# Regrouping the TensorE transposes of a step in a paged-attention and LoRA kernel

## What is computed

```python
q, k, v = x @ Wq.T, x @ Wk.T, x @ Wv.T          # 4 query heads, 1 key and 1 value head in a group
q, k = rope(rmsnorm(q, q_norm_w)), rope(rmsnorm(k, k_norm_w))
k_all, v_all = concat(k_cache[pages], k), concat(v_cache[pages], v)      # 512 + 128 keys
scores = where(valid, q @ k_all.T / sqrt(128), -1e30)
x = x + (softmax(scores) @ v_all) @ Wo.T
base, h, logits = x @ W.T, x @ A.T, x @ Wr.T + language_bias
gates = softmax(top2(logits))                   # spread over the 8 experts
x = x + base + 2.0 * (h * gates) @ B
```

## Time and profile before

| | before |
|---|---|
| median of 3 runs | 1166.06 us (1165.09 to 1166.17) |
| the profiled execution's own time | 1164.94 us |
| its span | 1163.1 us |
| TensorE busy | 1144.9 us, 98% of the span |
| ScalarE, VectorE, GpSimd busy | 80%, 79%, 66% |
| DMA, mean | 84 GB/s |
| mean granted TensorE clock | 0.997 of full speed |

### The profile page before, as it was taken

The page is one execution under the profiler, slowest core; times in us unless marked ns, Lnnn a source line. Parts: engine busy times, 40 slices in busy tenths (PEclk is TensorE's granted clock), DMA queues, the critical chain, the costliest instruction groups (busy, mean ns, idle before and its releaser), DMA issues.

```text
span 1163.1 us, 20954 instructions
## 1 busy us (share of the span) xinstructions
PE 1144.9 (98%) x6932; PEld 1025.0 (88%) x6932; DVE 918.5 (79%) x1884; ACT 931.8 (80%) x1832; POOL 768.7 (66%) x833
## 2 busy tenths in 40 slices
PE   7899999999999999999999999999999999999998
PEld 6788888889989989988998998899899899889887
DVE  7988888787788778778778877877877787787746
ACT  6888888888888888888888888888888888887741
POOL 5766766767776676776677677677766767766600
PEclk9899999999999999999999999999999999999999
DMA  7423332223222223222322222222232222221001
GB/s 235 158 74 100 122 104 84 64 87 88 77 79 92 81 68 91 89 68 87 91 78 73 91 89 64 87 89 73 82 91 81 67 89 88 64 78 56 19 1 73
DMA packets 56763, 98.12 MB, mean 84 GB/s; under 512 B 8784, under 2 KB 29136, under 8 KB 56528
## 3 DMA queue, kind: packets, MB, share of 16 engines
q1 hardware_dynamic: 44368, 63.21, 17.2%
q0 software_dynamic: 12288, 33.57, 10.1%
HBM read 90.45 MB, written 6.29 MB: 83 GB/s over the span
## 4 chain that ended last, share of the span: by engine, by line
PE 92%; DVE 3%; ACT 2%; issue 1%; DMA 0%; POOL 0%; SPq 0%; ACTq 0%; DVEq 0%; POOLq 0%
PE ps_w L306 19%; PE ps_w L308 18%; PE ps_w L307 18%; PE ps_s L1297 18%; PE ps_w L1306 9%; PE ps_w L1375 2%; PE ps_w L1273 2%; PE ps_w L1280 2%; PE ps_s L1214 1%; ACT ps L645 1%; PE ps_w L1246 1%; DVE m L868 0%; DVE w_lo L792 0%; DVE pt_lo L792 0%; DMA w_raw<-wqkv 0%
## 5 line engine op out<-in xcount | busy, mean ns | idle before, releaser
L466 POOL DMA_INDIRECT kv_raw<-kv,rows x256 | 255.6, 999 | 95.7 <-issue 62.2
L651 ACT ACTIVATE ps<-ps,recip 128x640 f32<-128x640 f32 x256 | 213.1, 832 | 64.0 <-DVE recip L902 64.0
L792 DVE TENSOR_TENSOR pt_lo<-ps_w,pt_hi 128x512 fp32r<-128x512 f32 x322 | 210.3, 686 | 67.7 <-ACT pt_hi L656 65.3
L645 ACT ACTIVATE ps<-ps,negmax 128x640 f32<-128x640 f32 x256 | 211.6, 827 | 38.9 <-DVE negmax L895 38.9
L895 DVE CUSTOM_DVE_ANT_0 ps<-ps_s,mask 128x640 f32<-128x640 f32 x256 | 210.3, 822 | 7.5 <-PE ps_s L1297 3.5
L656 ACT ACTIVATE pt_hi<-ps_w 128x512 fp32r<-128x512 f32 x256 | 152.7, 596 | 57.2 <-PE ps_w L1306 57.2
L306 PE MATMUL ps_w<-w_hi,xt_hi 128*128 128x512 f32 (+1 forms) x496 | 177.0, 357 | 1.6 <-DVE w_lo L792 1.4
L308 PE MATMUL ps_w<-w_hi,xt_lo 128*128 128x512 f32 (+1 forms) x496 | 167.1, 337 | 0.0
L307 PE MATMUL ps_w<-w_lo,xt_hi 128*128 128x512 f32 (+1 forms) x496 | 166.7, 336 | 0.0
L1306 PE MATMUL ps_w<-cst,ps 128*128 128x128 f32 x1024 | 154.1, 273 | 1.0 <-DVE w_lo L792 0.8
L484 POOL TENSOR_TENSOR rot<-u,cos 128x640 f32<-128x640 f32 x63 | 100.5, 1596 | 69.4 <-DVE u L940 69.4
(11 more groups left out here) (182 smaller groups left out, 2598.6 us busy)
## 6 DMA issues: line engine op xcount, KB each, us to landing
xt_hi<-xsplit SPq DMA_DIRECT2D x56, 256.0 KB, 2.8
xt_lo<-xsplit SPq DMA_DIRECT2D x56, 256.0 KB, 2.8
w_raw<-wqkv SPq DMA_DIRECT2D x56, 192.0 KB, 2.4
wo_raw<-wo SPq DMA_DIRECT2D x56, 128.0 KB, 2.2
kv_raw<-kv,rows POOLq DMA_INDIRECT x256, 2.9
y<-xT SPq DMA_DIRECT2D x8, 256.0 KB, 3.6
y<-x SPq DMA_DIRECT2D x8, 256.0 KB, 5.6
out<-y SPq DMA_DIRECT2D x8, 256.0 KB, 2.2
```

The source lines that it names most:

```text
L466: pool.indirect_dma_start(kv_raw[:, g % 2, t, :], None, kv[:, :], bass.IndirectOffsetOnAxis(rows[:, g % B, t:t + 1], 0)).then_inc(s_kv[g % ...
L645: nc.scalar.activation(ps[:, h, :], ps[:, h, :], ACT.Exp, bias=negmax[:, s % 2, h:h + 1], scale=-1.0, accum_out=rowsum[:, s % 2, h:h + 1]) ...
L651: nc.scalar.activation(ps[:, h, :], ps[:, h, :], ACT.Copy, scale=recip[:, s % 2, h:h + 1]).then_inc(a_norm, 1)
L792: return nc.vector.tensor_tensor(out_ap, full, hi.bitcast(F32), ALU.subtract)
```

## The change

The order of TensorE in a step becomes: scores 0 and 1, query projection, scores 2, O, scores 3, then T0, T1, T2 in one run, Y, then QT, KTC, KTN, T3, TN in one run, and the key and value projection last, no longer cut in two. The eight banks are dealt out anew: the twelve uses of `ps_w` become eleven with a list for each bank, and KTN goes into the last 128 columns of a score bank. In the new lists KV stands behind QT, T3 behind T2, TN behind Y, KTC behind T1 and T0 behind Q. ScalarE and VectorE take their copies and low parts in the new order: the values ahead of T0; T2 ahead of the exponential of head 3 on ScalarE and ahead of its reciprocal on VectorE; the piece of the next weights ahead of QT; the piece of the output weights behind TN. In the first step and in the last ones the corresponding places are moved as well. No instruction is added or removed, apart from waits.

```diff
-UNITS = ["Q", "O", "T0", "T1", "Y", "T2", "QT", "KTC", "KV", "KTN", "T3", "TN"]
-NU = len(UNITS)
-NBANK = 4
+BANKS = (("Q", "T0", "QT", "KV"), ("O", "Y", "TN"), ("T1", "KTC"), ("T2", "T3"))
+NBANK = len(BANKS)
...
+        def new_keys_bank():
+            return ps_s[:, 1, 1, 512 - S:512]
...
         def wait_bank(pe, s, unit):
 
-            n = UNITS.index(unit)
+            users = [users for users in BANKS if unit in users][0]
+            n = users.index(unit)
             while True:
-                n -= NBANK
+                n -= 1
                 if n < 0:
-                    n, s = n + NU, s - 1
+                    n, s = n + len(users), s - 1
...
                 if has(s):
-                    probs(0)
 
                     wait_kv(act, s)
                     wait(act, a_kv, s)
                     wait(act, pe_o, s - 1)
                     nc.scalar.activation(v_hi[:, 0:CT, :], kv_raw[:, s % 2, :, D:2 * D], ACT.Copy).then_inc(a_vhi, 1)
                     nc.scalar.activation(v_hi[:, CT, :], raw[:, s % 2, QW + D:WW], ACT.Copy).then_inc(a_vhi, 1)
-                if has(s):
+                    probs(0)
                     probs(1)
+                    probs(2)
...
-                if has(s):
-                    probs(2)
+                for n in W_AT.get(s, ()):
+                    w_split(n)
                 if has(g1):
                     turned_queries(g1)
                     cached_keys(g1)
-                for n in W_AT.get(s, ()):
-                    w_split(n)
-                if has(g1):
                     new_keys(g1)
...
                 if has(s):
                     probs(1)
+                    probs(2)
                     over_sum(3)
...
-                if has(s):
-                    turn_probs(0)
                 if has(s) and s >= G - HB + 1:
                     pe.wait_ge(d_xlo, B + s - (G - HB + 1) + 1)
                 if has(s):
                     scores(3)
+                    turn_probs(0)
                     turn_probs(1)
                 if s == 0:
                     project_keys_values(g2)
+                if has(s):
+                    turn_probs(2)
...
-                if has(s):
-                    turn_probs(2)
                 if has(g1):
                     turn_queries(g1)
                     turn_cached_keys(g1)
-                turn_x(s, "QT")
-                turn_x(s, "KTC")
-                half_layer(s, "KV")
-                if has(g2) and s > 0:
-                    project_keys_values(g2, new_keys_of=g1)
-                elif has(g1):
                     turn_new_keys(g1)
-                turn_x(s, "KTN")
+                for unit in ("QT", "KTC", "KTN"):
+                    turn_x(s, unit)
                 if has(s):
                     turn_probs(3)
+                    if s == 0:
+                        wait(pe, a_kv, g2)
                     wait_bank(pe, s, "TN")
                     for h in range(REP):
                         last = nc.tensor.transpose(bank("TN")[:, h * S:(h + 1) * S], ps[:, h, L:KEYS], ident)
                     last.then_inc(pe_tn, 1)
+                half_layer(s, "KV")
+                if has(g2) and s > 0:
+                    project_keys_values(g2)
```

More of the change, by code:

```diff
@@ L872, in turned_queries @@
                 wait(dve, a_qt, g)
-                low(qt_lo[:], bank("QT"), qt_hi[:]).then_inc(d_qt, 1)
+                low(qt_lo[:], queries_turned_bank(g), qt_hi[:]).then_inc(d_qt, 1)
             def cached_keys(g):
@@ L880, in new_keys @@
                 wait(dve, a_ktn, g)
-                low(kt_lo[:, L:KEYS], bank("KTN")[:, 0:S], kt_hi[:, L:KEYS]).then_inc(d_ktn, 1)
+                low(kt_lo[:, L:KEYS], new_keys_bank(), kt_hi[:, L:KEYS]).then_inc(d_ktn, 1)
             def step(s):
@@ L1168, in turn_x @@
                 wait(pe, d_y, G - B + c)
-                wait_bank(pe, s, unit)
+                if unit == "KTN":
+                    wait(pe, d_max, s, 4)
+                else:
+                    wait_bank(pe, s, unit)
                 for k in range(KC):
-                    last = nc.tensor.transpose(bank(unit)[:, k * S:(k + 1) * S], y[:, c, k * P:(k + 1) * P], ident)
+                    last = nc.tensor.transpose(x_turned_bank(unit)[:, k * S:(k + 1) * S], y[:, c, k * P:(k + 1) * P], ident)
                 last.then_inc(pe_xt, 1)
@@ L1241, in turn_new_keys, with project_keys_values @@
             def turn_new_keys(g):
-                if g == 0:
-                    wait(pe, a_kv, 0)
-                else:
-                    wait_bank(pe, g - 1, "KTN")
-                nc.tensor.transpose(bank("KTN")[:, 0:S], rot[:, REP, :], ident).then_inc(pe_ktn, 1)
-            def project_keys_values(g, new_keys_of=None):
+                nc.tensor.transpose(new_keys_bank(), rot[:, REP, :], ident).then_inc(pe_ktn, 1)
+            def project_keys_values(g):
                 if g == 1:
                     wait(pe, a_q, 0)
-                elif g >= 2:
+                elif g > 2:
                     wait_bank(pe, g - 2, "KV")
@@ L1256, in between @@
                         pe.wait_ge(d_wlo, k // 2 + 1)
-                    if new_keys_of is not None and k == KC - 1:
-                        turn_new_keys(new_keys_of)
                 wh, wl = head_weights(g // B)
@@ L1272, in turn_queries @@
                 for h in range(REP):
-                    last = nc.tensor.transpose(bank("QT")[:, h * S:(h + 1) * S], rot[:, h, :], ident)
+                    last = nc.tensor.transpose(queries_turned_bank(g)[:, h * S:(h + 1) * S], rot[:, h, :], ident)
                 last.then_inc(pe_qt, 1)
@@ L1303, in turn_probs @@
                     wait(pe, a_norm, s, 4, h + 1)
+                    if s == 0 and h == 2:
+                        wait(pe, a_q, 1)
                     wait_bank(pe, s, f"T{h}")
```

62 lines of the change are left out of this document (32 added, 30 removed).

## The result

The changed kernel takes 1176.61 us (median of four runs, 1175.82 to 1177.76), the kernel before 1166.05 us beside it (1165.09 to 1166.17). The ratio is 1.009, with a 95% interval of 1.0074 to 1.0106: slower by a little, clear of the noise, and close to the 1175.6 us forecast. So the traces show 12.3 us between the kernels and the medians 10.6.

A forecast was written before the change was run, and what follows sets the result against it. TensorE's own list was taken to bound the plain steps. Profiled 1164.94 - 1.0 (runs) + 10.9 (KV wait) + 0.4 (early steps) + 0.2 (step 62) - 1.0 (end) = 1174.4, so 1175.6 us on the median; range 1168.5 to 1190.

The forecast's parts named there:

- The chain from QT to the projection: QT's transposes, ScalarE copy, VectorE low part, then KV: 1.99 us against TensorE's own 1.78, a 0.21 us wait per step.
- The runs: Three fewer runs of transposes a step: 0.02 us saved, bounds 0.00 to 0.06; 1.0 us faster over 52 steps.
- Steps 1 to 4: KV waits for QT's low part behind extra VectorE work: 1.5 us in step 2, about 0.9 in each other.
- Steps 5 to 9: KV waits 0.2 to 0.7 us each, where weight pieces stand ahead of head 3's exponential; 1.7 us together.
- the term for products at half clock in step 1: TensorE products at half clock in step 1 add 0.9 us, within the early steps' net +0.4.
- Step 62: Half a second layer stands in KV's place with the same wait: +0.2 us.
- The end: Step 63: T3's bank is free, so 0.9 us goes, with 0.1 more at TN: -1.0, bounds 0 and -1.5.
- ScalarE at QT: ScalarE's weight piece ends by 605.81, QT's copy is due at 605.77: just in time, hardly any slack.
- (c): Rival: ScalarE reaches QT late; 0.2 us late doubles KV's wait to about 0.4, 1186 us; chance 0.08.
- Where it shows: KV's first product should show about 0.2 us idle per step put down to VectorE's qt_lo; steps 17.25 us.
- (b): Rival: no KV wait if the chain from QT takes under 1.78 us; 1163, up to 1165 us; chance 0.12.
- (d): Rival: the longer transpose run lowers TensorE's clock; at 1 us a step, near 1228 us; chance 0.02.

The follow-up runs named there:

- score bank kernel: Changed kernel with the key and value projection written into a score bank: 1175.94 us (first chip), 1171.00 (second), 1159.51 (third; kernel before 1164.67).
- kernel of two runs more: The score bank kernel with T0 ahead of head 3's scores again and KTN alone inside Y: 1176.48 us (first chip), 1170.66 (second).

## Why the prediction was right, step by step

- **The method held.** TensorE's list sets the step, so the 52 steps from 10 to 61 carry the result: they hold 12.6 us, and the rest of the traces' 12.3 cancels to -0.3.
- **That the number is so close is in part luck.** The sum was made for the profiled execution, and there it gave 1174.4 us against 1177.23, 2.8 too low. On the medians only 1.0 is left of that, because the profiled execution of the kernel before lay 1.1 us under its median and that of the changed one 0.6 above. And within the 2.8, steps 10 to 61 were 2.7 too low and the rest cancels.
- **The chain from QT to the projection** was put at 1.99 us and took 2.01; TensorE's own 1.78 us took 594.71 to 596.49, 1.78. The wait was 0.24 us instead of 0.21, inside its bounds of 0.15 and 0.35. That is 0.03 x 52 = 1.6 us of the 2.8.
- **A term that was missing:** the projection's products are 0.02 us slower behind a wait (1.535 against 1.514 us), 1 us in 52 steps. Together with the wait it makes the step 17.30 instead of 17.25.
- **The runs** were put at 0.02 us a step; the score bank kernel has exactly the change's lists without the wait and takes 17.040 against 17.056, so 0.016, and 17.053 on the first chip, so next to nothing. Inside its bounds of 0.00 and 0.06, and as small as it was said to be.
- **Steps 1 to 4** were put at 4.2 us of waits for the projection. TN's time to the next start was 1.26, 1.67, 1.38 and 1.32 us there, less 0.355 each: 4.2. Steps 5 to 9 waited 0.33 and four times 0.24, 1.3 us, not 1.7. The sum for steps 1 to 9 came out at +0.96 for +0.4, within its bounds. What was too small is the term for products at half clock in step 1: the scores of heads 0 and 1 took 3.34 us at a granted clock of 0.50, before 2.69 at 0.65, and 1.76 in a plain step. The forecast had 0.9 us there; it was about 1.7.
- **Step 62** was wrong in sign: -0.49 for +0.2. Before, TensorE lost time there ahead of Y (the four transposes ahead of it took 0.80 us to the next start) and ahead of the next scores (0.62), 0.45 and 0.27 us over the usual 0.355; both are gone, against an added wait of 0.33. I had looked only at the wait that was added and not at those that go.
- **The end** came out at -1.1 for -1.0.
- **ScalarE at QT** wasn't just in time, as worked out from the earlier trace rows, but 0.26 us early by its starts, of which the profile shows 0.17 as idle. The division ended 0.09 us sooner behind QT's start than worked out (0.05 for 0.14), the piece started 0.10 ahead of the division's end, and the next copy could start 0.09 ahead of the piece's. The forecast named early starts of this kind and didn't count them. This slack is what kept rival (c) away.
- **Where it shows.** I said the first product of the projection would show idle time for qt_lo. The group of products shows 2.5 us in all; the rest is behind modelled ends and stands in the row of the weight loads (16.5 us), and in full only in the starts.

**The rivals.** (b), no wait, is out: the chain takes 2.01 us against the 1.78 it decides at. The score bank kernel shows what (b) would have looked like: 5.2 us under the kernel before, where I gave it 3. (c), a second delay through ScalarE, didn't come; with 0.36 us of work added on ScalarE it came, by 0.07 us a step. (d), the clock, is out: the granted clock of the plain steps is 1.00 of the 2.4 GHz level in the changed kernel, runs of seventeen transposes with a wait behind them included. The Trainium skill, "TensorE: Matmul & The Clock Gate", section "Part 4: PE-mode transpose", has transposes not count as work for the clock; at this share of a step the trace shows no harm from it.

**A rule that bore on the change.** The trace shows a product held up by the reader of a bank that was filled 2 us earlier, and the same product in another bank not held up at all. The Trainium skill, "Perfetto Trace Analysis", section "Matmuls", asks that independent groups rotate through different banks so that the reading of one lies beside the matmuls of the next. The traces of both kernels agree. What decides here isn't the number of banks but how many us of TensorE's own work stand between two users of one: 1.78 against 2.01.

## What to carry to other kernels

Here regrouping transposes saved hardly anything by itself (at most 0.014 us a run), so cost a reordering by its waits: for each unit that moves, take the distance in time to the unit ahead of it and behind it in its bank, and compare it with the time in which both readers are done. On an engine whose ends are modelled, small waits are read from the starts of equal steps, not from its busy share. And two orders can change places from one chip to the next: compare them on more than one.

## What was not expected of the hardware

- VectorE on two of three chips starts one instruction late against all that the trace shows it to need: by 0.8 us in about every other step of the kernel before, by 0.2 to 1.9 in nearly every step of the changed and the score bank kernel. The kernel before takes 23 to 28 us longer there (1189.47 and 1192.27 against 1166.05 and 1164.67).
- Starts on ScalarE come about 0.1 us before the end of the last instruction, so an added copy of 0.46 us takes 0.36.
- A product whose start was held up costs its group 0.02 us more than the wait: 1.535 us against 1.514 for twelve.
- The first scores of step 0, behind 1.59 us of idle time on TensorE, can be at the lower clock in one execution and not in another: in the changed kernel's profiled execution on the third chip they took 0.53 us for two products (granted clock 0.52 from 24 to 26 us), in the score bank kernel's there 0.29 (1.00). With what followed that is 1.5 us more of the span. The kernel of two runs more had it in one of its two profiled executions (0.50 against 1.00 from 24 to 26 us).
